# An adaLN mixture-of-experts block on one core: the layer norm's subtraction from ScalarE to VectorE, and a new order of the first stage

## The reference

```python
mod = (silu(c) @ wmod).reshape(2, 6, 1, -1)
sa, ca, ga, sb, cb, gb = (mod[:, n] for n in range(6))
ga = (2 * (ga >= 0) - 1) * maximum(abs(ga), 0.25)      # the same for gb
h = layernorm(x) * (1 + ca) + sa
x = x + ga * (h + attention1(h @ W.T + b))             # 16 heads of 16, causal
h = layernorm(x) * (1 + cb) + sb
x = x + gb * ffn(h)                                    # a second attention, then a mixture of 8 experts
```

## Time and profile before

| | us |
|---|---|
| median of 3 runs | 3002.18 (2999.23 to 3015.74) |
| the profiled execution, its time | 3015.74 |
| the profiled execution, its span from first to last instruction | 3013.9 |
| TensorE busy | 2773.6 |
| VectorE busy | 2058.9 |
| ScalarE busy | 1549.1 |
| GpSimd busy | 1216.3 |

### The profile page before, as it was taken

How to read it: one execution, slowest core, us unless ns; L and a number is a source line. 1 busy time by engine, 2 the same in 40 slices (tenths; PEclk the granted TensorE clock), 3 DMA queues, 4 the chain that set the end, 5 groups by cost and what they waited for, 6 DMA issues and landing times. The chain is left out here.

```text
span 3013.9 us, 47433 instructions
## 1 busy us (share of the span) xinstructions
PE 2773.6 (92%) x18752; PEld 1776.2 (59%) x18752; DVE 2058.9 (68%) x3294; ACT 1549.1 (51%) x3205; POOL 1216.3 (40%) x371
## 2 busy tenths in 40 slices
PE   6689999999999967868999999999999999599998
PEld 5544444444454345645666666666666665488887
DVE  7567888788888268757677677676767672355655
ACT  3335777677777622223455454545555555344442
POOL 5400000000000065523788887979797978000000
PEclk8856999899999879978999999999999999699999
DMA  6830330342140057682161313131313110223221
GB/s 180 238 46 3 49 49 10 44 75 27 26 63 7 6 188 243 201 210 53 25 137 39 64 36 68 32 70 30 71 29 71 29 33 5 70 95 106 85 92 64
DMA packets 144046, 223.63 MB, mean 74 GB/s; under 512 B 30928, under 2 KB 76112, under 8 KB 139536
## 3 DMA queue, kind: packets, MB, share of 16 engines
q1 hardware_dynamic: 143584, 220.21, 29.8%
q10 hardware_dynamic: 240, 0.39, 0.1%
HBM read 138.11 MB, written 81.92 MB: 73 GB/s over the span
## 5 line engine op out<-in xcount | busy, mean ns | idle before, releaser
L1511 ACT ACTIVATE a_prob<-a_pS 128x512 f32<-128x512 f32 (+3 forms) x1280 | 630.1, 534 | 583.9 <-PE a_pS L1593 276.1
L1492 POOL TENSOR_TENSOR a_zsum<-a_zsum,a_prob 128x2048 f32<-128x2048 f32 (+1 forms) x194 | 856.1, 4413 | 58.0 <-ACT a_prob L1511 31.9
L639 DVE TENSOR_REDUCE a_rowmax<-a_pR 128x2 f32<-128x1024 f32 (+3 forms) x640 | 652.2, 1061 | 140.2 <-PE a_pR L675 86.8
L620 ACT ACTIVATE a_prob<-a_pS 128x512 f32<-128x512 f32 (+3 forms) x1280 | 591.7, 539 | 277.7 <-PE a_pS L697 170.1
L1530 DVE TENSOR_REDUCE a_rowmax<-a_pR 128x2 f32<-128x1024 f32 x384 | 462.5, 1224 | 133.3 <-PE a_pR L1575 129.6
L1592 PE MATMUL a_pS<-a_q,a_key 128*128 128x512 f32 (+3 forms) x1280 | 505.3, 395 | 23.0 <-ACT a_prob L1511 16.3
L1593 PE MATMUL a_pS<-a_q,a_key 65*128 65x512 f32 (+3 forms) x1280 | 472.8, 369 | 0.0
L1575 PE MATMUL a_pR<-a_key,a_q 128*128 128x512 f32 (+3 forms) x1280 | 395.9, 393 | 34.9 <-DMA a_q<-mid_q 22.1
L697 PE MATMUL a_pS<-a_q,a_key 49*128 49x512 f32 (+3 forms) x1280 | 406.9, 451 | 11.8 <-DMA a_q<-a_neg 6.3
L675 PE MATMUL a_pR<-a_key,a_q 48*128 48x512 f32 (+3 forms) x1280 | 335.4, 459 | 21.4 <-PEq L2309 14.5
L1592 PEld LDWEIGHTS a_pS<-a_q,a_key 128*128 128x128 f32 x1280 | 246.3, 192 | 148.5 <-ACT a_prob L1511 57.8
(11 more groups left out here) (237 smaller groups left out, 3941.3 us busy)
## 6 DMA issues: line engine op xcount, KB each, us to landing
a_q<-mid_q SPq DMA_DIRECT2D x192, 256.0 KB, 7.1
a_key<-mid_qk SPq DMA_DIRECT2D x48, 256.0 KB, 9.1
a_q<-mid_qk SPq DMA_DIRECT2D x48, 256.0 KB, 15.1
e_spread<-mid_comb SPq DMA_DIRECT2D x8, 1536.0 KB, 6.3
mid_qk<-p_qk_hi SPq DMA_DIRECT2D x32, 256.0 KB, 5.1
mid_qk<-p_qk_lo SPq DMA_DIRECT2D x32, 256.0 KB, 5.7
mid_q<-p_n_hi SPq DMA_DIRECT2D x32, 256.0 KB, 3.1
mid_q<-p_n_lo SPq DMA_DIRECT2D x32, 256.0 KB, 3.9
```

Of the source, the lines that this page charges most:

```text
L620: act.activation(prob[:, n % 4, h, at:GT], pS[:, (HG * n + h) % NS, at:GT], ACT.Exp).then_inc(exp_ready, 1)
L639: dve.tensor_reduce(rowmax[:, c % 2, :, j, t, kc], pR[:, bank, :, 0:n], axis=AX.X, op=ALU.max).then_inc(r_read, 1)
L1492: pool.tensor_tensor(zsum[:, ring, :, at:GT], zsum[:, ring, :, at:GT], prob[:, step % 4, :, at:GT], ALU.add).then_inc(z_added, 1)
L1511: act.activation(prob[:, n % 4, h, at:GT], pS[:, (HG * n + h) % NS, at:GT], ACT.Exp, scale=SCALE).then_inc(exp_ready, 1)
```

## The change

1. **C and D.** ScalarE's four activations are gone. VectorE's C now ends with four `tensor_scalar` over 128x256, (x - mean) * rstd, with both scalars read per partition. D on VectorE is one `tensor_tensor` over 128x1024 with the scale row; D on GpSimd is an addition of the shift, of the same shape as the subtraction.
2. **Fills.** GpSimd's first four fills stand behind U(2), behind a wait for gate 5; the second four stay behind U(3).
3. **Order.** At the start mod 0 and 1 come ahead of B(0), and mod 2 to 5 come together ahead of W and T(0). In the loop T(n+1) stands behind Q3 of block n where it stood behind Q1. The x(1) load is issued ahead of wmod 1. TensorE's Q waits once for all six `mod_read`.

```diff
-            items = [("silu", 0), ("B", 0), ("C", 0), ("mod", 0), ("D", 0), ("W", 0), ("mod", 1), ("B", 1), ("mod", 2), ("T", 0)]
-            items += [("mod", 3), ("C", 1), ("mod", 4), ("gate", 2), ("D", 1), ("U", 0)]
+            items = [("silu", 0)] + [("mod", k) for k in range(2)] + [("B", 0), ("C", 0), ("D", 0), ("B", 1)]
+            items += [("mod", k) for k in range(2, 6)] + [("W", 0), ("T", 0), ("C", 1), ("gate", 2), ("D", 1), ("U", 0)]
             for n in range(BLOCKS):
-                steps = [("Q", n, 0), ("B", n + 2), ("Q", n, 1), ("T", n + 1), ("C", n + 2), ("Q", n, 2), ("D", n + 2), ("Q", n, 3)]
-                steps += [("mod", 5)] * (n == 0) + [("V", n, 0), ("V", n, 1), ("U", n + 1)]
+                steps = [("Q", n, 0), ("B", n + 2), ("Q", n, 1), ("C", n + 2), ("Q", n, 2), ("D", n + 2), ("Q", n, 3),
+                         ("T", n + 1), ("V", n, 0), ("V", n, 1), ("U", n + 1)]
...
+            load_x(1)
             load_wmod(1)
-            load_x(1)
...
-            fill(range(4))
-            pool.wait_ge(filled, 4)
...
-                    pool.tensor_tensor(h[:, n % HS], spread(b, 0), h[:, n % HS], ALU.subtract).then_inc(h_ready, 1)
+                    pool.tensor_tensor(h[:, n % HS], h[:, n % HS], spread(b, 0), ALU.add).then_inc(h_ready, 1)
...
-                    if n == 3:
+                    if n == 2:
                         pool.wait_ge(gates_ready, 2)
                         pool.wait_ge(w_ready, 1)
+                    if n in (2, 3):
                         pool.wait_ge(u_ready, n + 1)
-                        fill(range(4, 8))
-            pool.wait_ge(filled, 8)
+                        fill(range(4 * (n - 2), 4 * (n - 2) + 4))
+                        pool.wait_ge(filled, 4 * (n - 1))
...
-                if step == "C":
-                    if n >= HS:
-                        act.wait_ge(u_ready, n - HS + 1)
-                    for t in range(NTILE):
-                        last = act.activation(h[:, n % HS, t, :], x[:, n % XS, t, :], ACT.Identity, scale=-1.0, bias=mv[:, n % 2, t, 0:1])
-                    last.then_inc(centred, 1)
...
-                    if n >= 2:
-                        dve.wait_ge(centred, n - 1)
...
+                    dve.wait_ge(rstd_ready, n + 1)
+                    if n >= HS:
+                        dve.wait_ge(u_ready, n - HS + 1)
+                    for t in range(NTILE):
+                        last = dve.tensor_scalar(h[:, n % HS, t, :], x[:, n % XS, t, :], mv[:, s, t, 0:1], rstd[:, s, t:t + 1],
+                                                 ALU.subtract, ALU.mult)
+                    last.then_inc(unit_ready, 1)
...
-                    for t in range(NTILE):
-                        last = dve.scalar_tensor_tensor(out=h[:, n % HS, t, :], in0=h[:, n % HS, t, :], scalar=rstd[:, s, t:t + 1],
-                                                        in1=m.mod[:, b, 1, :], op0=ALU.mult, op1=ALU.mult)
-                    last.then_inc(scaled, 1)
+                    dve.wait_ge(unit_ready, n + 1)
+                    dve.tensor_tensor(h[:, n % HS], h[:, n % HS], spread(b, 1), ALU.mult).then_inc(scaled, 1)
...
-                    if n == 0:
-                        pe.wait_ge(mod_read, g + 1)
+                        pe.wait_ge(mod_read, len(MODS))
```

More of the change, by code:

```diff
@@ L80, in project1 @@
         w_high, w_ready, cast, filled = sem("w_high"), sem("w_ready"), sem("cast"), sem("filled")
-        stats_ready, aggr_ready, var_ready, sd_ready, rstd_ready, centred, scaled, h_ready = (
-            sem(n) for n in ("stats_ready", "aggr_ready", "var_ready", "sd_ready", "rstd_ready", "centred", "scaled", "h_ready"))
+        stats_ready, aggr_ready, var_ready, sd_ready, rstd_ready, unit_ready, scaled, h_ready = (
+            sem(n) for n in ("stats_ready", "aggr_ready", "var_ready", "sd_ready", "rstd_ready", "unit_ready", "scaled", "h_ready"))
         gated, u_ready, t_psum, hi_ready, lo_ready = (sem(n) for n in ("gated", "u_ready", "t_psum", "hi_ready", "lo_ready"))
@@ L289, in _ @@
                         dve.wait_ge(mod_read, 1 + b)
-                    dve.wait_ge(rstd_ready, n + 1)
-                    dve.wait_ge(centred, n + 1)
-                    for t in range(NTILE):
-                        last = dve.scalar_tensor_tensor(out=h[:, n % HS, t, :], in0=h[:, n % HS, t, :], scalar=rstd[:, s, t:t + 1],
-                                                        in1=m.mod[:, b, 1, :], op0=ALU.mult, op1=ALU.mult)
-                    last.then_inc(scaled, 1)
+                    dve.wait_ge(unit_ready, n + 1)
+                    dve.tensor_tensor(h[:, n % HS], h[:, n % HS], spread(b, 1), ALU.mult).then_inc(scaled, 1)
                 if step == "T":
@@ L357, in _ @@
                         pe.wait_ge(v_read, 2 * n + g - 1)
-                    else:
-                        pe.wait_ge(mod_read, RING + g + 1)
                     for t in range(2):
```

## The result

| | before | after |
|---|---|---|
| first comparison, median us | 3006.9 (6 runs) | 3035.26 (6 runs) |
| second | 3010.26 (29) | 3024.63 (6) |
| third | 3011.76 (35) | 3027.42 (12) |
| ratio, 95% interval | | 1.007 [1.0044, 1.0096]; 1.0058 [1.0037, 1.0079]; 1.0037 [1.0014, 1.0061] |
| span of the profiled execution | 3013.9 | 3025.3 |

The account below looks back on a forecast made before the run. It saw TensorE busy for 2773.6 of 3013.9 us, the first stage set by its load circle and DMA tail. Load x(6) +5.8, less 1.15, about +4.6, taken as +5 on 3002.2: 3007 us, range 2992 to 3021.

Parts of the forecast that it names:

- What bounds the stage: First stage: its DMA-saturated tail moves with the loop feeding it; delaying GpSimd's U delays a later load and its D.
- Start: Before the first Q: the wait for mod weights spends most of the free GpSimd's gain; first Q +0.9 us.
- Shape of C and D: VectorE in each block: +0.8 us of work, but B to D shortens by 1.15 us where the x load decides.
- T behind Q3: Loop, T(n+1) behind D and Q3: nothing lost where a load sets the pace, elsewhere some 1.5 us.
- serial chain: Loop, from D through Q3, T and Q0 to the next block's B and D: 12.7 us a block.
- Fills: Four memsets behind U(2), 14.2 us, hold D(4)'s addition on GpSimd: U(3) ends 5.8 us later, at 86.9.
- third rival: VectorE and GpSimd take turns: memsets repeatedly hold C's tensor_scalar; +10 to +11 us, up to +20; chance 0.18.
- the sum: Stage end: x(6) load +5.8 us, D(6) gets back 1.15, about +4.6; taken as +5 us.
- hidden move: Rival: DMA backlog before the tail hides the fills' delay; -4 to +1 us, 2998 to 3003; chance 0.17.

Follow-up runs that it names:

- the run: Changed kernel with T(n+1) moved back behind Q1: attention1 began at 157.5 us, ratio 1.0046 [1.0022, 1.007].
- pure delay: Kernel before plus three GpSimd memsets of 32x4096 ending the first stage, run twice: attention1 at 157.3 and 155.2 us, ratios 1.0044 and 1.0036.

## Why the prediction was wrong, by its steps

*What bounds the stage* held in its shape. The tail moved with the loop (share 1.00, 306 GB/s), and the load behind U's store carried the delay on: U(3) at 89.8, x(6) issued at 93.3, 3.5 us later. It doesn't move one for one: U(6) was 10.7 us later and the stage's end 9.4, and where C and D alone were changed the last stretch, from U(6) to `attention1`, was 2.5 to 3.8 us shorter than before's.

*Start*: +0.9 was forecast; against the two profiles of before the first Q is 2.1 to 3.2 us later (27.2 and 28.0 against 25.1 and 24.8), though before's own four profiles spread from 23.5 to 26.2. The term left out the table load of 1.28 us. The Trainium skill, "ScalarE: Activation LUTs", section "What ACT_TABLE_LOAD costs", has about 1283 ns for one, and this trace agrees; I had its row at hand in the trace and didn't ask where the load would go once mod reads stood between exponential and root. The larger error was of view: I wrote that most of the free start is spent on the mods, and took that as given. It is a part of the change with a price of its own. Alone in the kernel before it costs the stage 3.1 to 5.4 us (149.7 against 144.3 to 146.6); in the changed kernel 5.7 to 7.9 (153.9 to 156.0 against 148.2).

*Shape of C and D*: sizes right. Four `tensor_scalar` took 1.38 us (forecast 1.2), the `tensor_tensor` 1.22 (1.3). Without late fills it costs loop and tail nothing: 119.4.

*T behind Q3*: the serial chain was forecast at 12.7 us for a block; U(3) to U(6) took 128.2 - 89.8 = 38.4, 12.8 each. It isn't a loss against T behind Q1, as the run shows.

*Fills*: the mechanism was right, its size too small. Forecast was U(3) 5.8 us later; it came 8.7 later. Of the 2.9 us between, 0.5 is the later start of the memsets and 2.4 GpSimd's wait for D(4). I let C of block 4 be held once and end at 73.8; it was held by three memsets in turn and ended at 80.67. That was my third rival, which gave 80.6 for C and 82.7 for D(4) (82.5 in the trace), and I had left it a chance of 0.18. The Trainium skill's rule of the exclusive lock ("SBUF — State Buffer", section "SBUF: two separate sides"), which the prediction cites, is borne out once more. That this rival's +10 to +11 us is near the measured stage is luck in part: with C on ScalarE and no such turns the loop and tail lost nearly as much (127.5), and with the turns added they didn't get longer (127.0).

*The step that failed* is the sum: "D(6) gets back 1.15: about +4.6". It let the load of x(6) decide when block 6 begins. In the changed kernel it doesn't:

```profile
93.28 0.48 SPq L109 DMA_DIRECT2D p_x<-in_x_dram  x1
...
100.69 1.40 DVE L266 BATCH_NORM_STATS2 p_stats<-p_x 128x6 f32<-128x256 f32 x4
...
106.76 1.22 DVE L289 TENSOR_TENSOR p_h<-p_h,mod 128x1024 f32<-128x1024 f32 x1
```

The load is issued 8.8 us later than before, not 5.8. The path from B to D did shorten as forecast, 7.29 us in place of 8.35. But B(6) no longer waits for the DMA; it starts 7.4 us behind the issue of its load, where it was 6.2, because VectorE's own chain from D(4), held to 82.5, is now last. So the 1.1 us gained were lost again, and D(6) ended at 107.98, 8.9 us later in place of 4.6.

The fills' term was thus mis-sized in what is carried on. It measured 6 to 8 us with C on ScalarE and 8 to 10 in the changed kernel (loop and tail with and without late fills), in place of 4.1. The chain's pace of 12.8 us a block, where before took 12.1 in the mean (81.1 to 117.5), is not by itself the loss: with the fills at the start the same three blocks took 12.6 each (82.8 to 120.5) in a stage with no loss in loop and tail, and with late fills and C on ScalarE they took 12.1 and 6 us were lost all the same. The stage's 9.4 is 2.1 at the first Q and 7.3 behind it.

*The total*: the stage is +10 us of it, the ratios stand for +11 to +21, and the medians moved by +14 to +28. At the same clock the changed kernel costs what a pure delay of its size costs. The rest goes with a lower mean clock, and what lowered it is open; the forecast had no term for it. The base was part of the miss too: I started from a median of three, 3002.2, and the kernel before later had medians of 3006.9 to 3013.2, so a range up to 3021 had less room than it seemed. Its lower end, 2992, is the middle of the hidden move less 8.25; from that rival's end of 2998 it would be 2990.

## What to carry to other kernels

Look for a place for a later stage's work where its engine's queue has nothing behind it that someone waits for: here at the very start until the first inputs land (two memsets, first Q at 22.0), or behind the last item. All four at the start cost the first Q some 4 us. A quiet engine in the middle of a loop wasn't such a place, since its short idle gaps lay between steps that others waited for, and four gaps cost as much as one. When steps that come once are moved together for order's sake, write down for each engine what now stands ahead of the first result, table loads too. And where a program's executions spread by 20 us, judge a 5 us edit by the stage's own end in more than one trace, and compare totals at the same mean clock before you call a rest unexplained.

## What the runs showed of the hardware

- Four independent `tensor_scalar` of 128x256, 1.38 us alone, took 9.48 us beside memsets of 3.5 us (8.29 in two other versions); beside memsets of 0.6 us they took 2.36 and 2.56, and beside GpSimd's `tensor_tensor` of 2.4 us 1.84 or 3.78. VectorE doesn't keep its turn over a row of them: in the changed kernel memsets ended at 73.0, 76.6 and 80.2, and one `tensor_scalar` got through at each of these ends, the second starting at 73.07 and the third at 76.67.
- Not every operation of VectorE is held. Beside the same memsets its four `scalar_tensor_tensor` with two inputs in SBUF (L292, C on ScalarE) took 1.66 us, as ever; beside GpSimd's `tensor_tensor`, L263 with two inputs took 2.74 for 0.69.
- Mean granted clock and time go together over executions of one program: 3002.42 us at 0.941 and 3021.2 at 0.934, and over 133 executions 2.0 us for each 0.001. In every profile the clock is at its lower level, 1.2 GHz, for parts of the first 150 us of `attention1` (granted 0.50 from 155 to 165 us in each); what sets when it rises again isn't shown here.
